# Spreading the row pairs of the last phase: eight in the first four steps, 32 over the other twenty, and four pairs loaded plainly ahead

## The reference

```python
x = _layernorm(x + _L0_gnn_ref(x, edge_index, edge_attr_64, ...))   # edge MLP, segment sum, dense MLP
x = _layernorm(x + _L1_gnn_ref(x, edge_index, ...))                 # mean of neighbours, batch norm, leaky relu, + x
x = _layernorm(x + _L2_gnn_ref(x, src, dst, ...))                   # equivariant messages on edges, segment sum
x = _layernorm(x + _L3_gnn_ref(x, batch0, edge_index, L3_gnn_W))    # attention over the edges of a node
```

## Time and profile before

| | |
|---|---|
| median of 3 runs | 2155.74 us |
| profiled execution | 2156.94 us, its span 2155.2 us |
| PE busy | 1803.9 us (84%) |
| DVE busy | 1434.7 us (67%) |
| ACT busy | 1149.2 us (53%) |
| POOL busy | 949.1 us (44%) |
| mean granted PE clock | 0.896 |

### The profile page before, as it was taken

The page is one execution under the profiler, slowest core; times in us unless marked ns, Lnnn a source line. Parts: engine busy times, 40 slices in busy tenths (PEclk is TensorE's granted clock), DMA queues, the critical chain, the costliest instruction groups (busy, mean ns, idle before and its releaser), DMA issues. The chain is left out here.

```text
span 2155.2 us, 24520 instructions
## 1 busy us (share of the span) xinstructions
PE 1803.9 (84%) x5525; PEld 933.2 (43%) x5525; DVE 1434.7 (67%) x2621; ACT 1149.2 (53%) x2356; POOL 949.1 (44%) x1070
## 2 busy tenths in 40 slices
PE   5999999599999999999999995961881588998840
PEld 2444444244444444444444443531771344544420
DVE  5365554177777777777777773517995578787876
ACT  1344434255555555555555552224883878877853
POOL 2212102166666666656666663544553232333236
PEclk8999999799999999999999997985555689999965
DMA  7752102534444454444444445554556887878774
GB/s 250 250 206 63 27 13 31 142 134 172 171 159 166 157 172 172 165 164 155 169 172 172 163 153 188 105 87 156 110 119 178 257 242 221 238 212 241 200 212 144
DMA packets 167421, 350.61 MB, mean 163 GB/s; under 512 B 30481, under 2 KB 30962, under 8 KB 166838
## 3 DMA queue, kind: packets, MB, share of 16 engines
q1 hardware_dynamic: 130838, 247.28, 32.4%
q0 software_dynamic: 33168, 98.01, 20.4%
q10 hardware_dynamic: 3344, 4.51, 0.7%
HBM read 177.32 MB, written 153.71 MB: 154 GB/s over the span
## 5 line engine op out<-in xcount | busy, mean ns | idle before, releaser
L687 PE MATMUL d_p_h<-w3a,d_xT 128*128 128x512 f32 x632 | 285.6, 595 | 23.2 <-DMA d_xT<-in_xT 23.2
L687 PE MATMUL d_p_p<-d_wr,d_x1T 128*128 128x512 f32 x632 | 288.3, 600 | 0.0
L687 PE MATMUL d_p_o<-d_w,d_uT 128*128 128x512 f32 x632 | 284.5, 593 | 3.0 <-ACT d_uT L762 3.0
L562 POOL TENSOR_SCALAR d_small<-d_mv 128x1 f32<-128x1 f32 x158 | 77.6, 491 | 296.7 <-DVE d_mv L813 148.7
L851 DVE TENSOR_TENSOR d_zz<-d_yg,d_xbeta 128x512 f32<-128x512 f32 x79 | 136.9, 1733 | 96.3 <-POOL d_yg L902 96.3
L687 PEld LDWEIGHTS d_p_h<-w3a,d_xT 128*128 128x128 f32 x632 | 120.7, 191 | 175.6 <-issue 175.6
L687 PEld LDWEIGHTS d_p_o<-d_w,d_uT 128*128 128x128 f32 x632 | 119.8, 190 | 153.7 <-issue 149.1
L755 ACT ACTIVATE d_yn<-d_y,d_small 128x512 f32<-128x512 f32 x79 | 64.3, 814 | 228.2 <-POOL d_small L567 228.2
L687 PEld LDWEIGHTS d_p_p<-d_wr,d_x1T 128*128 128x128 f32 x632 | 115.6, 193 | 116.5 <-issue 116.5
L783 ACT ACTIVATE d_x<-d_zz,d_small 128x512 f32<-128x512 f32 x79 | 64.2, 813 | 174.9 <-POOL d_small L567 174.9
L294 PE MATMUL m_p_H<-m_xT,m_w 128*128 128x512 f32 x320 | 146.8, 613 | 4.8 <-ACT m_xT L335 4.8
(11 more groups left out here) (286 smaller groups left out, 4080.9 us busy)
## 6 DMA issues: line engine op xcount, KB each, us to landing
sum_counted<-m_tile_sum SPq DMA_DIRECT2D x10, 2112.0 KB
state<-d_empty SPq DMA_DIRECT2D x80, 264.0 KB, 2.4
update<-d_empty SPq DMA_DIRECT2D x80, 256.0 KB, 2.3
pair_x<-x SPq DMA_DIRECT2D x40, 512.0 KB
out_rows<-pair_rows SPq DMA_DIRECT2D x40, 512.0 KB
d_xT<-in_xT SPq DMA_DIRECT2D x79, 256.0 KB
d_z<-sum_counted SPq DMA_DIRECT2D x79, 256.0 KB
d_x<-in_x SPq DMA_DIRECT2D x79, 256.0 KB
```

The lines of the kernel that those rows point to most:

```text
L562: nc.gpsimd.tensor_scalar(tmp, var, factor, add, ALU.mult, ALU.add).then_inc(done, 1)
L687: last = nc.tensor.matmul(out[:, :], lhsT[:, c, :], w[:, c, :], start=(c == 0), stop=(c == KB - 1))
```

## The change

`plain_plan` gives 2 pairs to each of the steps 0 to 3, and 2, 2, 1, 1, 2 in each group of five steps from 4 to 23 (before: 3, 3, 2, 2, then 2 and 1 in turn to step 21, then 1 and 2). `PLAIN` goes from 3 to 4, so pair 3 is loaded plainly in the edge-rows phase and has the extra shift on DVE, and the fill that was issued there for it is gone. `tile_plan` and its cap of three are as they were.

```diff
-PLAIN = 3
+PLAIN = 4
...
-    plan = [3, 3, 2, 2] + [2 - i % 2 for i in range(steps - 6)] + [1, 2]
+    plan = [2] * 4 + [2, 2, 1, 1, 2] * ((steps - 4) // 5)
     assert sum(plan) == PAIRS
...
 def pair_fill(nc, k, sp, j):
 
     b = j % ROW_BUFS
-    if j >= ROW_BUFS:
-        sp.wait_ge(k.pair_gone[b], 16 * (j // ROW_BUFS))
-    else:
-        sp.wait_ge(k.quotient_done, 1)
+    sp.wait_ge(k.pair_gone[b], 16 * (j // ROW_BUFS))
...
             for j in range(2):
                 pair_load_x1(nc, k, sp, j)
-            pair_fill(nc, k, sp, PLAIN)
             sp.wait_ge(scattered, 16 * T)
...
                 if step + 1 < STEPS:
-                    for j in range(given, given + HERE[step + 1]):
+                    for j in range(max(given, PLAIN), given + HERE[step + 1]):
                         pair_add_p(nc, k, pool, j)
```

## The result

The changed kernel takes 2258.92 us (median of three runs, 2256.26 to 2264.07) against 2155.74: 4.7% slower, ratio 1.0473 with a 95% interval of 1.0431 to 1.0515. The forecast was 2289 us in a range of 2245 to 2335, so the direction and the place were right and the size was 30 us too large. Its profiled execution has a span of 2257.2 us, 102.0 more than before.

A forecast was written before the change was run, and what follows sets the result against it. Before, merge-to-pair and DVE work bound the loop, 37.3 us per two steps; afterwards the merged buffer chain. Last pair 2217.8 plus 1.3 rule shortfall, 68.1 attention rows and 1.7 around the span gave 2289 us, range 2245 to 2335.

The forecast's parts named there:

- The walk: Loop steps computed one by one from link times read in the old trace; last pair done at 2217.8 us.
- the rule for a late start: One-pair step on DVE: its merge ends 13.7 us after its pair's late start.
- the three links store, fill and waited add: Row buffer's chain after ACT's tile: 3.8 us store to fill, 4.9 fill to add, 6.1 add to pair's start.
- shorter links as a side case (2255 us): Buffer chain in stalled steps: with a store of 2.7 us, last pair done at 2184, so 2255 us.
- a rival (2200 to 2250, 7 in 100): Short links keep the loop's stalls partly covered: 2250 us or less, down to 2200; chance 0.07.
- the main forecast: Merged chain in the loop's steps sets the pace: 2250 to 2330 us, chance 0.80.
- The two chains, beside each other until now, become one: Loop: POOL waiting in an add can't scatter, joining the state's chain to the buffer's; 118 us behind at step 23's merge.
- Before no add stood in a step ahead of the ACT step that frees its buffer: Count over both tables of POOL's adds ahead of ACT's freeing step: none before, ten after.
- the list: Adds said to stand ahead of ACT's freeing step: pairs 19, 25, 27, 31, 33, 34, 35, 36, 37 and 39.
- The fill's 15 us: First steps: eight pairs instead of ten before the first merge, ending near 1715 instead of 1730.29; 15 us gained.
- The rival of a lower granted clock: TensorE's pauses in stalled steps lower its clock: 8.7 us a step, 44 us over five, 2333 us; chance 0.08.
- the listed signs: POOL's fill waits over 200 us, merge wait halved, DVE's add waits over 100, step 20 longest, late loss, unchanged end.

The follow-up runs named there:

- The five buffers: Changed kernel with five row buffers instead of four, pair 4 also loaded plainly and small changes to make room; ACT's cap of three kept: 2160.0 us, ratio 1.0025.
- its control: The kernel before, old table, with ACT's cap at four tiles a step instead of three and nothing else: 2182.0 us, ratio 1.0131.
- the two other parts of the change: Changed kernel with old table, four plain pairs: 2155.8 us, 1.0000; changed kernel with new first four steps, old alternation, then 2 and 3 pairs: 2156.2 us, 1.0002.

## Why the prediction was right, and where it was not

**The cause.** The prediction said that ACT falls behind in runs of two-pair steps and frees buffers after the add that needs them. The five buffers (1.0025) and the cap of four beside its control (1.0096 and 1.0131) show it from two sides; the two other parts of the change cost nothing that can be told (1.0000 and 1.0002).

**The walk.** The rules, taken from a few steps of the trace before, gave merge ends of 1715, 1833, 1858, 1879, 1917, 1942, 1970 and 2000 for steps 4, 10, 11, 12, 14, 15, 16 and 17; measured are 1714.6, 1832.4, 1852.9, 1880.1, 1917.1, 1939.6, 1967.0 and 1996.6. Part of this closeness is luck, since errors cancel in it:

```profile
1852.20 0.70 DVE L2044 TENSOR_TENSOR f_new<-f_new,f_part 128x520 f32<-128x520 f32 x1
...
1863.12 1.22 DVE L1250 TENSOR_TENSOR pair_rows<-pair_rows,bn_scale 128x1024 f32<-128x1024 f32 x1 [10.22 <-DMA pair_rows<-p_rows]
...
1879.36 0.70 DVE L2044 TENSOR_TENSOR f_new<-f_new,f_part 128x520 f32<-128x520 f32 x1
```

The walk let a merge end 14.4 us after POOL's scatter at the earliest; step 11's ended 12.3 us after it (1840.61 to 1852.90), and the walk had it 5 us too late. The one-pair step that followed took 16.9 us from its pair's start (1863.12 to 1880.06) where the rule for a late start has 13.7, and so the walk was right again at step 12. Beyond step 17 it runs off: 2081 against 2069.9 at step 20, 2134 against 2116.2 at 21, 2196 against 2166.8 at 23.

**The term that was mis-sized** is first of all the sum of the three links store, fill and waited add: 14.8 us in the prediction (3.8, 4.9, 6.1). At step 20 it was 11.9 (2.7, 3.6, 5.6). Over all the adds that stood ahead of their tile's step it was 13.1 in the mean (11.8 to 16.7, from the end of the tile to the pair's start): 1.7 less each, and with eleven of them (see the count below) 19 us of the 29 by which the last pair came earlier than predicted (2188.7 against 2217.8). A second term was off the same way: the one-pair steps 21 and 22 took 11.5 us from their pair's late start to the merge's end instead of 13.7, 4.4 us together. Step 21:

```profile
2131.66 1.22 DVE L1250 TENSOR_TENSOR pair_rows<-pair_rows,bn_scale 128x1024 f32<-128x1024 f32 x1 [15.41 <-DMA pair_rows<-p_rows]
...
2142.47 0.70 DVE L2044 TENSOR_TENSOR f_new<-f_new,f_part 128x520 f32<-128x520 f32 x1
```

Both are estimates of shares, since not every link lies wholly on the path. The same rule of 13.7 us erred the other way in steps 11, 16 and 17 (16.9 to 17.2 us), so how the rest of the 29 us comes about stays open. The prediction had shorter links as a side case (2255 us) and as a rival (2200 to 2250, 7 in 100); the result lies between that rival and the 2289, inside the main forecast's 2250 to 2330 but near its low end. The reason given there, fewer transfers in flight, fits what the rows show but is not shown by itself. The share of the transfer engines' time, last but one in these window rows (changed kernel from 1900 us on, then the kernel before over its last loop steps; columns as above),

```profile
1900.00:2180.00 280.00, 173.81 (x536) 96.29 (x534) 146.36 (x280) 144.85 (x390) 51.63 (x48) 0.77 0.54 155
```

```profile
1900.00:2087.00 187.00, 157.20 (x541) 85.73 (x539) 143.63 (x274) 139.65 (x377) 55.41 (x49) 0.90 0.76 218
```

fell from 0.76 to 0.54, and the adds' landing in the same two stretches, again first in the changed kernel and then before, is

```profile
DMA to landing us min/median/max: 5.4/5.8/7.4
```

```profile
DMA to landing us min/median/max: 7.6/8.2/9.0
```

But most of that difference was in the prediction's rules already: it took 8.5 us for an add right behind the gathers and 6.1 for one that POOL had waited in, and in the changed kernel most adds are of the second kind. Like for like, the waited add went from 6.1 to 5.6 at step 20.

**What was wrong in the mechanism.** "The two chains, beside each other until now, become one" put part of the cost on POOL's blocked scatter. With most of that blocking gone (155 us of late scatters down to 48) nothing comes back (1.0510), and DVE waited only 2.7 us for the old state. The walk came out near all the same because in it the same chain also holds DVE's pairs.

**A wrong count.** "Before no add stood in a step ahead of the ACT step that frees its buffer" does not hold for the first steps: the old table has three such adds, of pairs 4 and 5 in step 0 and of pair 7 in step 1. Their waits for fills are 14.06, 7.25 and 6.59 us, and they may be part of why the new fill is ahead at step 4. For the steps after them there are none before, as said, but eleven after and not ten: pair 28 is missing from the list. Its add stands in POOL's step 15, and the tile that frees its buffer is the first of ACT's step 16. In the trace that tile ends at 1967.59, after the merge at 1967.04, and the add waits 10.30 us for its fill. The walk's 1970 and 2000 fit a stall there, so the miscount may lie in the list alone.

**The fill's 15 us** were there (15.7), and as the prediction said they hardly mattered: in the changed kernel the merges are level by step 12. That they can't be kept even with the old loop, since two pairs are put off to the end, was not seen.

**The clock.** The rival of a lower granted clock had its condition fulfilled, and no price shows. The clock fell to 0.77 in the stalled part (0.90 before, rows above), and the product behind step 20's first pair took as long as the slow one of the earlier trace rows:

```profile
2091.42 2.10 PE L1802 MATMUL f_p_S<-f_both,same_src 128*128 128x260 f32 x4 [10.67 <-DVE f_both L2013]
...
2096.96 6.72 PE L1758 MATMUL f_p_qv<-filters,same_dst 128*128 128x512 f32 x8 [1.73 <-ACT same_dst L1838]
2113.62 0.38 PE L1776 MATMUL f_p_k<-ident,scores 128*8 128x128 f32 x1 [9.94 <-DVE scores L1987]
```

TensorE then sat idle for 9.94 us waiting for DVE. The slower product lay in a pause that was there anyway. Nor did DVE wait longer for TensorE over the phase: its waits for products came to 29.7 us in the kernel before and to 7.4 us in the changed one. The longest of each, before and then after:

```profile
DVE same_dst L1989 <- PE f_p_k L1762: 14.3, 8, 2.7
```

```profile
DVE same_dst L1985 <- PE f_p_k L1758: 3.6, 3, 1.7
```

No run here changed the clock alone, so that it cost nothing is read from such rows, not shown.

**What would show it.** All of the listed signs came: fills over 200 us (249.5), the merge's wait under half (28.7), adds over 100 (149.4), step 20 the longest with 46.3 us, the merge of step 10 ahead of 1844 (1832.4) and the loss in the second half, the end with its 68 us.

## What to carry to other kernels

When a table gives a pipeline its work, write down for each buffer the step in which it is freed and the step in which it is needed, on the engines that do each; a limit elsewhere (here three tiles a step on ACT) can make the new table owe work that the old one did not, and the stall is then the whole chain of release, store, refill and restart. A queue that waits inside such a chain looks like the cause in the waits; moving the blocked instruction tests whether it is. Before raising the limit instead, measure the limit's own effect as a control: here a higher limit cost 28 us of its own with the old table, and so brought back some 83 of the 103 us and not all.

## What the runs showed of the hardware

The landing of a 512 KB accumulating add was 8.2 us (median of 15, 7.6 to 9.0) in the kernel before from 1900 us on, with the transfer engines 76% busy, and 5.8 us (median of 17, 5.4 to 7.4) in the changed kernel from 1900 us on, with 54%. Their load is not all of it: in the kernel before between 1640 and 1900 us the engines were 82% busy and the median was lower, 7.4 us (6.0 to 9.7). What stands ahead of the add counts too. In the kernel before, where DVE was waiting for the add, it took 5.7 to 6.9 us from issue to the pair's start in the seven cases in which POOL had waited for the fill, and 6.2 to 10.0 us (median 8.6) in the eight in which the add was issued right behind the gathers. No run here parts the two causes.

So a link's time that is read in the busy part of a kernel can be too long for the same link in a stall: the chain of store, fill and add was put at 14.8 us from such rows and measured 11.9 at step 20, 13.1 in the mean of eleven.
